# Linear attention and gated feed-forward on one core: the first chunk taken alone, and other tiles for the norms and first folds

## The chip, the cores and the metric

The kernel runs on one core of one Trainium2 chip. The metric is the device time of one execution in microseconds (us). The kernel before took 1321.6 us, the median of three runs (1320.43 to 1321.61 us).

## The reference

The input is x, 8 chunks of 512 tokens with 512 features. Every token is normalised, the attention branch forms three projections and a running sum over the tokens, the feed-forward branch runs between Hadamard transforms (fwht), and the two meet in a gate:

```python
xn = (x - mean) / sqrt(var + 1e-5)
q, k, v = xn @ Wq.T + bq, xn @ Wk.T + bk, xn @ Wv.T + bv
phi_q, phi_k = elu(q) + 1, elu(k) + 1
s = (phi_q * cumsum(phi_k * v, tokens)) * SCALE @ Wo.T + bo
y = fwht(xn * SU_ug) / 64
h = silu(y @ W_gate.T * ws_gate * 64) * (y @ W_up.T * ws_up * 64)   # 2048 wide
z = (fwht(h * SU_dp) / 64) @ W_down.T * (ws_down * 64)
out = x + s * silu(z)
```

## The kernel before

The eight chunks are taken in four pairs (`PAIRS`). Operands are split into two float16 halves, HI and LO, and a product is the sum of HI·HI, HI·LO and LO·HI, so that the result is near float32. The Hadamard transforms are folded into the weights of gate, up and down, on the chip, while the first pair runs.

A pair runs through 22 groups: K, V, Q, K, V, Q and then eight times gate and up. A group of the first pair (`first_group`, on every engine) is four tiles of 128x512, numbered 0 to 87 through the groups as 4g + j; tile j of a group has the weight rows `ROW_OF[j]` and the chunk `CHUNK_OF[j]`. A tile of the first pair is twelve matmuls (`plain_tile`, line 1542): six with kk=0, then six with kk=1. Later pairs use seven products for a group (line 1641), in the Winograd manner. After the groups come the down products (line 1719) and the attention output (line 1751).

The order on each engine is the order of the code; semaphores tie the engines. What the change and the prediction touch:

- **SyncE** loads x of the first two chunks (line 518, four tiles each, `ident` between the chunks), then Wk, Wv and Wq (line 523), constants, and the eight blocks of gate and up (line 530).
- **VectorE** takes the statistics (lines 970 and 985), the inverse root by Newton steps (lines 995 to 1002), and normalises (line 1008). `weight_scale` (lines 949 to 1156) makes a power-of-two scale from a weight's bound; `attn_low` (line 1167) writes the LO half of a piece of weights, which is what `piece_made` counts and what a group of TensorE waits for. `first_x_low` (line 1032) writes LO of the tokens.
- **ScalarE** squares the attention weights (`square_attn`, line 673) for that bound, writes HI of a piece (`attn_high`, line 705) and HI of the tokens (`first_x_high`, line 680), squares the gate and up blocks (`square`, line 712), and takes the tiles of K and Q (exp at line 799, relu at line 802). `square(i)` has two buffers: it waits until the norm of block i-2 is done.
- **TensorE** transposes the normalised tokens (line 1677), runs the tiles, sums the squares of block i in `norm(i)` (line 1561, 16 small matmuls), and folds the Hadamard signs into gate and up (`fold(n, second)`, lines 1575 and 1577; with q = 2(n-6) + second). A tile waits until the tile four before it has been taken out of its bank.
- **Bounds and folds of gate and up** on VectorE: `read_norms` (line 1207), after all eight norms; `scale_gate_up` (lines 1218 to 1223); the additions of the transform, `fly_rows` (lines 1259 and 1260, 1.2 us each); `fold_low` (line 1268), the LO half of what TensorE folds; `scale_hidden` (lines 1228 to 1240); `ug_low` (line 1174), the LO half of a folded piece. The HI halves are ScalarE's `fold_high` (line 742) and `ug_high` (lines 728 and 733).

At which tile each of these stands is said by tables (`FLY_AT`, `FOLD_HIGH_AT`, `FOLD_LOW_AT`) and by conditions in `first_weights` and in the two `first_group` functions. On VectorE the work of a tile is `use`: one feature for K (line 1075), product and scan for V (lines 1085 and 1090), feature and context for Q (lines 1075 and 1099).

Of the kernel before, what the change touches and what calls it, by code (L numbers as in the profile page):

```python
# [8 lines left out]
I32 = mybir.dt.int32  # L9
ALU = mybir.AluOpType  # L10
# [55 lines left out]
FIRST_TOKENS = {B11: 0, B21: 1, B12: 2, B22: 3}  # L66
# [32 lines left out]
FLY_AT = {6: (0, 0), 7: (0, 1), 10: (1, 0), 11: (1, 1)}  # L99
FOLD_HIGH_AT, FOLD_LOW_AT = {(14, 0): 0, (15, 1): 0}, {(15, 0): 0, (17, 1): 0}  # L100
for _i in range(1, FP):
    if _i >= 2:
        FLY_AT[8 * _i + 8], FLY_AT[8 * _i + 9] = (_i, 0), (_i, 1)
    FOLD_HIGH_AT[8 * _i + 11, 0], FOLD_HIGH_AT[8 * _i + 15, 1] = _i, _i
    FOLD_LOW_AT[8 * _i + 13, 0], FOLD_LOW_AT[8 * _i + 16, 1] = _i, _i

# [61 lines left out]
def build(nc, x, x_t, wk_t, wv_t, wq_t, wo_t, ug_t, down_t, vecs, rows, ident_in, hada_in, signs_in, out):  # L168
# [6 lines left out]
    with ExitStack() as ctx_stack:  # L175
# [111 lines left out]
        x_made, x_ready = sem("x_made"), sem("x_ready")  # L287
# [123 lines left out]
        def tile_in(eng, p, g, j):  # L411

            if p == 0:
                eng.wait_ge(plain_done, 4 * g + j + 1)
                return plain_bank(g, j)[:, :]
            if j == C21:
                eng.wait_ge(product_done, products_to(p, g, P4))
                return chain_bank(g)[:, :]
            eng.wait_ge(summed, 3 * nth(p, g) + (1, 2, 0, 3)[j])
            return tile(g, j)  # L420

        @block.sync
        def _(sp):
# [92 lines left out]
            for c in FIRST_CHUNKS:  # L516
                for t in range(TB):
                    sp.dma_start(x_ln[:, TB * c + t, :], x[c, t * P:(t + 1) * P, :]) \
                        .then_inc(x_first_loaded[TB * c + t], 16)
                if c == FIRST_CHUNKS[0]:  # L520
                    sp.dma_start(ident[:, :], ident_in).then_inc(ident_loaded, 16)
            for m, w in ((K, wk_t), (V, wv_t), (Q, wq_t)):
                sp.dma_start(raw_attn[m], w).then_inc(attn_raw_loaded[m], 16)
                if m == K:
                    sp.dma_start(vec[:, :], vecs).then_inc(vec_loaded, 16)
# [54 lines left out]
        def _(pool):  # L580
# [3 lines left out]
            def rstd_of(p):  # L584
                pool.wait_ge(var_ready, p)
                pool.tensor_tensor(rstd[:, :], var_eps[:, :], minus_half[:, :], ALU.pow).then_inc(rstd_ready, 1)
# [48 lines left out]
            for m in (K, V, Q):  # L635
                pool.wait_ge(attn_squared, m + 1)
                all_max(m, m + 1).then_inc(attn_bounded, 1)
            load_blocks(0)
# [29 lines left out]
        def _(act):  # L668
# [7 lines left out]
            def first_x_high(a):  # L676
                kk, b = FIRST_BLOCKS[a]
                act.wait_ge(xp_done, 4 if a < 4 else 8)
                src = bank[(R_BANK if kk else D_BANK)[FIRST_TOKENS[b]]]
                act.activation(xops[:, kk, HI, b, :], src[:, :], ACT.Copy).then_inc(x_hi, 1)  # L680
# [154 lines left out]
            def first_group(g):  # L835
                for j in range(4):
# [11 lines left out]
                    if j in (1, 3) and QKV_GROUPS <= g + 2 < GROUPS:  # L848
                        ug_high(g + 2, j // 2)
# [37 lines left out]
            for a in range(8):  # L887
                first_x_high(a)
            square_attn(V)
            square_attn(Q)  # L890
            attn_high(1)
# [33 lines left out]
        def _(dve):  # L925
# [41 lines left out]
            def first_stats():  # L967
                for t in [TB * c + t for c in FIRST_CHUNKS for t in range(TB)]:
                    dve.wait_ge(x_first_loaded[t], 16)
                    last = dve.bn_stats(stats[:, t, :], x_ln[:, t, :])  # L970
                prep.after(last)
                variances(0)
# [10 lines left out]
            def variances(p):  # L983
                for t in range(2 * TB):
                    last = dve.bn_aggr(mean_var[:, t, :], stats[:, t, :])
                prep.after(last)
                last = dve.tensor_scalar(var_eps[:, :], mean_var[:, :, 1], EPS, None, ALU.add)
                if p:
                    last.then_inc(var_ready, 1)
                else:  # L990
                    prep.after(last)

            def first_inverse_root():

                prep.after(dve.tensor_scalar(newton[:, :].bitcast(I32), var_eps[:, :].bitcast(I32), 1, None,
                                             ALU.logical_shift_right))
                prep.after(dve.tensor_scalar(rstd[:, :].bitcast(I32), newton[:, :].bitcast(I32), -1.0,
                                             float(INVERSE_ROOT_BITS), ALU.mult, ALU.add))
                for _ in range(NEWTON_STEPS):
                    prep.after(dve.scalar_tensor_tensor(newton[:, :], rstd[:, :], -0.5, rstd[:, :], ALU.mult, ALU.mult))  # L1000
                    prep.after(dve.tensor_tensor(newton[:, :], newton[:, :], var_eps[:, :], ALU.mult))
                    prep.after(dve.scalar_tensor_tensor(rstd[:, :], newton[:, :], 1.5, rstd[:, :], ALU.add, ALU.mult))

            def scale_root():
                prep.after(dve.tensor_scalar(rstd[:, :], rstd[:, :], X_SCALE, None, ALU.mult))

            def normalise(t):
                dve.tensor_scalar(x_ln[:, t, :], x_ln[:, t, :], mean_var[:, t, 0:1], rstd[:, t:t + 1],
                                  ALU.subtract, ALU.mult).then_inc(xn_ready, 1)

            def means_and_roots(p):
                dve.wait_ge(rstd_ready, p)
                if p > 1:
                    dve.wait_ge(mean_root_stored, 16 * (p - 1))
                dve.tensor_scalar(mean_root[:, 0, :], mean_var[:, :, 0], 1.0, None, ALU.mult)
                prep.after(dve.tensor_scalar(mean_root[:, 1, :], rstd[:, :], X_SCALE, None, ALU.mult))  # L1016
                dve.sem_inc(mean_root_made, 1)
# [10 lines left out]
            def first_x_low(a):  # L1028
                kk, b = FIRST_BLOCKS[a]
                src = bank[(R_BANK if kk else D_BANK)[FIRST_TOKENS[b]]]  # L1030
                dve.wait_ge(x_hi, a + 1)
                last = dve.tensor_tensor(xops[:, kk, LO, b, :], src[:, :], xops[:, kk, HI, b, :], ALU.subtract)  # L1032
                if a % 4 == 3:
# [352 lines left out]
            def first_weights(g, part):  # L1386
# [3 lines left out]
                if g == 2 and part == 3:  # L1390
                    read_norms()
                if 4 * g + part in FLY_AT:
                    i, level = FLY_AT[4 * g + part]
                    fly_rows(i, level)
                if g == 3:
                    if part == 1:
                        scale_gate_up()
                    elif part == 3:
                        fold_low(0, 0)
                        scale_hidden()  # L1400
                else:
                    for m in range(2):
                        if (4 * g + part, m) in FOLD_LOW_AT:
                            fold_low(FOLD_LOW_AT[4 * g + part, m], m)
                if part == 0 and QKV_GROUPS <= g + 1 < GROUPS:
                    ug_low(g + 1, True)
                if part == 2 and QKV_GROUPS <= g + 2 < GROUPS:
                    ug_low(g + 2, False)
# [59 lines left out]
            first_stats()  # L1468
            first_inverse_root()
            scale_root()  # L1470
            for t in range(TB):
                normalise(TB * FIRST_CHUNKS[0] + t)
            weight_scale(K)
            for t in range(TB):
                normalise(TB * FIRST_CHUNKS[1] + t)
            attn_low(0)
            for a in range(8):
                first_x_low(a)
            weight_scale(V)
            attn_low(1)  # L1480
# [55 lines left out]
        def _(pe):  # L1536
            def plain_tile(g, j):
# [3 lines left out]
                for n, (kk, dh, s, xs) in enumerate(terms):  # L1541
                    mm = pe.matmul(plain_bank(g, j)[:, :], at[:, s, 2 * dh + kk, r, :],  # L1542
# [48 lines left out]
            def first_group(g):  # L1591
                pe.wait_ge(piece_made, g + 1)
                for j in range(4):
                    if g == 0 and j < 2:
                        pe.wait_ge(x_ready, j + 1)
                    wait_plain_bank(g, j)
                    plain_tile(g, j)
                    n = 4 * g + j - (2 if g == 0 else 3)
                    if (2 if g else 0) <= n < FP:
                        norm(n)  # L1600
                    if QKV_GROUPS <= g + 2 < GROUPS and j in (0, 2):
                        fold(g + 2, j // 2)
# [67 lines left out]
            def first_transposes():  # L1670
                for a, c in enumerate(FIRST_CHUNKS):
                    for t in range(TB):
                        pe.wait_ge(xn_ready, TB * a + t + 1)
                        for k in range(KB):
                            dh, kk = divmod(k, 2)
                            to = bank[(R_BANK if kk else D_BANK)[2 * c + dh]]
                            mm = pe.transpose(to[:, t * P:(t + 1) * P], x_ln[:, TB * c + t, k * P:(k + 1) * P],
                                              ident[:, :])
                            if t == TB - 1:
                                mm.then_inc(xp_done, 1)  # L1680
# [76 lines left out]
            first_transposes()  # L1757
# [62 lines left out]
```

## Time and profile before

| | |
|---|---|
| median of three runs | 1321.6 us |
| profiled execution | 1322.33 us |
| its span | 1320.5 us |
| TensorE busy, matmul | 1283.2 us (97%) |
| VectorE busy | 887.5 us (67%) |
| ScalarE busy | 542.6 us (41%) |
| GpSimd busy | 63.1 us (5%) |
| mean granted TensorE clock | 0.996 |

Busy shares are means over stages with different limits. The span starts with the first instruction and the rest of the time, 1.8 us, lies around it. The times of the timeline are from the span's start. An engine's idle time stands in brackets behind the instruction that ended it, with what released it.

### The profile page before, as it was taken

What the parts mean: (1) busy time and instruction counts of PE and PEld (TensorE: products, weight loads), DVE (VectorE), ACT (ScalarE), POOL (GpSimd) and SP (SyncE); (2) the same over time, 40 slices, a digit from 0 to 9 for tenths busy, and PEclk for the clock granted to TensorE, in tenths of its full rate; (3) what the DMA queues carried; (4) which work ended last, traced back from release to release, by engine and by line L of the source; (5) the groups of instructions that cost most, each with busy time, mean ns of one, the idle gap of its engine ahead of it and who ended that gap; (6) DMA issues with size and microseconds to landing.
All of it is one profiled execution on the core that took longest, in us unless ns stands there. A gap on an engine that the chain in (4) does not pass through costs nothing.

```text
span 1320.5 us, 15902 instructions
## 1 busy us (share of the span) xinstructions
PE 1283.2 (97%) x6004; PEld 581.5 (44%) x6004; DVE 887.5 (67%) x1367; ACT 542.6 (41%) x819; POOL 63.1 (5%) x108
## 2 busy tenths in 40 slices
PE   4989999999999999999999999999999999999998
PEld 3434444444444444444444444444444444444443
DVE  6889999978776777767725755566754674455423
ACT  5855665640125655441114554442112654443000
POOL 1000111121000010110000000010000000000000
PEclk9989999999999999999999999999999999999999
DMA  9512443578765366644545323334444323323230
GB/s 364 231 56 88 175 158 145 181 245 307 186 261 178 126 212 234 204 148 132 208 140 191 128 96 128 119 136 160 159 160 162 126 100 124 128 98 126 98 126 32
DMA packets 54508, 210.44 MB, mean 159 GB/s; under 512 B 12064, under 2 KB 12320, under 8 KB 37792
## 3 DMA queue, kind: packets, MB, share of 16 engines
q1 hardware_dynamic: 45888, 180.07, 38.4%
q0 software_dynamic: 8544, 29.37, 6.7%
q8 instruction: 47, 0.77, 0.2%
q14 instruction: 29, 0.24, 0.1%
HBM read 164.30 MB, written 45.11 MB: 159 GB/s over the span
## 4 chain that ended last, share of the span: by engine, by line
PE 57%; DVE 3%; issue 2%; ACT 2%; DMA 1%; DVEq 0%; ACTq 0%
PE bank L1641 34%; PE bank L1719 19%; PE bank L1751 4%; DMA h_all<-scr_f 1%; ACT work L799 1%; DVE work L1085 1%; ACT work L802 1%; DVE work L1069 0%; DVE work L1108 0%; DVE work L1075 0%; DVE h_all L1117 0%; ACT h_all L756 0%; ACT work L789 0%; ACT L799 0%; DVE h_all L1202 0%
## 5 line engine op out<-in xcount | busy, mean ns | idle before, releaser
L1641 PE MATMUL bank<-xops,ring 128*128 128x512 f16 x2772 | 602.7, 379 | 7.5 <-DVE work L1069 2.9
L1641 PEld LDWEIGHTS bank<-xops,ring 128*128 128x128 f16 x2772 | 269.5, 98 | 339.7 <-issue 9.8
L1719 PE MATMUL bank<-ring,h_all 128*128 128x512 f16 x1536 | 333.3, 379 | 1.4 <-DMA ring<-scr_d 1.4
L1069 DVE TENSOR_TENSOR work<-bank,work 128x512 f32<-128x512 f32 x198 | 133.8, 686 | 164.7 <-PE bank L1641 150.9
L1542 PE MATMUL bank<-xops,ring 128*128 128x512 f16 x1056 | 239.4, 382 | 5.0 <-DVE xops L1032 2.7
L1719 PEld LDWEIGHTS bank<-ring,h_all 128*128 128x128 f16 x1536 | 150.2, 98 | 182.9 <-DMA ring<-scr_d 1.9
L789 ACT ACTIVATE work<-bank 128x512 f32<-128x512 f32 x198 | 117.8, 595 | 243.9 <-PE bank L1641 243.2
L1542 PEld LDWEIGHTS bank<-xops,ring 128*128 128x128 f16 x1056 | 103.1, 98 | 135.4 <-issue 14.8
L883 ACT ACTIVATE gate_g<-gate_g 128x512 f32<-128x512 f32 x32 | 19.9, 630 | 252.3 <-DVE gate_g L1349 252.3
L819 ACT ACTIVATE h_all<-work 128x512 f16<-128x512 f32 x128 | 77.9, 624 | 68.6 <-DVE work L1108 68.3
L1349 DVE TENSOR_TENSOR gate_g<-bank,row 128x512 f32<-128x512 f32 x32 | 21.4, 688 | 115.6 <-PE bank L1719 115.0
L1117 DVE TENSOR_TENSOR h_all<-work,h_all 128x512 f16<-128x512 f32 x128 | 87.4, 686 | 5.9 <-ACT h_all L819 4.7
L1751 PE MATMUL bank<-ring,ctx 128*128 128x512 f16 x384 | 84.2, 379 | 0.0
L1075 DVE SCALAR_TENSOR_TENSOR work<-work 128x512 f32<-128x512 f32 x64 | 44.1, 690 | 57.0 <-ACT work L802 56.8
L1751 PEld LDWEIGHTS bank<-ring,ctx 128*128 128x128 f16 x384 | 37.6, 98 | 45.3
L812 ACT ACTIVATE work<-bank,gate_out 128x512 f32<-128x512 f32 x56 | 38.0, 683 | 37.4 <-PE bank L1542 37.3
L812 ACT ACTIVATE work<-work,gate_out 128x512 f32<-128x512 f32 x72 | 51.0, 714 | 5.4 <-DVE work L1069 5.1
L1108 DVE SCALAR_TENSOR_TENSOR work<-work,up_out 128x512 f32<-128x512 f32 x72 | 52.2, 744 | 0.7 <-DVE mean_root L1016 0.4
L1108 DVE SCALAR_TENSOR_TENSOR work<-bank,up_out,work 128x512 f32<-128x512 f32 x56 | 41.8, 746 | 16.0 <-PE bank L1641 11.4
L1090 DVE TENSOR_TENSOR_SCAN work<-work 128x512 f32<-128x512 f32 x32 | 39.2, 1224 | 1.1
L799 ACT ACTIVATE work<-work,vec,i_attn 128x512 f32<-128x512 f32 x36 | 29.1, 807 | 9.6 <-DVE work L1069 9.5
L1358 DVE SCALAR_TENSOR_TENSOR s_f<-bank,o_out,row 128x512 f32<-128x512 f32 x32 | 23.9, 747 | 11.6 <-PE bank L1751 11.6
(172 smaller groups left out, 868.9 us busy)
## 6 DMA issues: line engine op xcount, KB each, us to landing
ring<-scr_g SPq DMA_DIRECT2D x66, 1024.0 KB, 4.8
ring<-scr_d SPq DMA_DIRECT2D x32, 1024.0 KB, 5.0
scr_g<-ring SPq DMA_DIRECT2D x22, 512.0 KB, 2.7
h_all<-in_ug_t SPq DMA_DIRECT2D x8, 1024.0 KB, 15.0
x_res<-in_x SPq DMA_DIRECT2D x32, 256.0 KB, 3.9
out<-x_res SPq DMA_DIRECT2D x32, 256.0 KB, 6.9
scr_g<-ring POOLq DMA_DIRECT2D x12, 512.0 KB, 4.1
work<-in_x_t SPq DMA_DIRECT2D x6, 1024.0 KB, 7.3
```

Of the source, the lines that this page charges most:

```text
L789: act.activation(tile(g, j), chain_bank(g)[:, :], ACT.Copy).then_inc(copied, 1)
L799: act.activation(exp_tile(n), src, ACT.Exp, bias=vec[:, b + f:b + f + 1], scale=i_attn[:, m:m + 1])
L812: act.activation(tile(g, j), src, ACT.Silu, scale=gate_out[:, at:at + 1]).then_inc(act_tiles, 1)
L819: act.activation(h[:, i, TILE_OF[j], HI, :], tile(g, j), ACT.Copy).then_inc(h_hi, 1)
L1069: dve.tensor_tensor(tile(g, j), at[:, :], tile(g, j), ALU.add).then_inc(summed, 1)
L1075: dve.scalar_tensor_tensor(tile(g, j), exp_tile(n), 1.0, tile(g, j), ALU.min, ALU.add) \
L1108: dve.scalar_tensor_tensor(tile(g, j), src, up_out[:, at:at + 1], tile(g - 1, j), ALU.mult, ALU.mult).then_inc(h_made, 1)
L1117: dve.tensor_tensor(at[:, LO, :], tile(g, j), at[:, HI, :], ALU.subtract).then_inc(h_ready, 1)
L1542: mm = pe.matmul(plain_bank(g, j)[:, :], at[:, s, 2 * dh + kk, r, :], xops[:, kk, xs, PLAIN_B[dh][c], :], start=(n == 0), stop=(n == len(t ...
L1641: mm = pe.matmul(to[:, :], weight_of(slot, s, b, kk), xops[:, kk, xs, c, :], start=(a == 0 and m in (P1, P2, P5)), stop=(a == 5), skip_gro ...
L1719: mm = pe.matmul(bank[D_BANK[t]][:, :], at[:, s, cols], w[:, :, ws, :], start=(a == 0 and b == 0 and n == 0), stop=(a == KB - 1 and b == K ...
L1751: mm = pe.matmul(bank[R_BANK[t]][:, :], at[:, s, cols], o_weight(slot)[:, f, ws, :], start=(n == 0), stop=(n == 3 * KB - 1))
```

## The change

**Loads.** SyncE issues the first chunk's four tiles, `ident`, then Wk, and only then the second chunk's four tiles, `vec`, Wv and Wq.

**First chunk alone.** VectorE takes the statistics of chunk 0 only, its inverse root, and normalises it; the scale of Wk; then the statistics of chunk 1, `attn_low(0)`, the LO halves of chunk 0, and only then normalises chunk 1. The inverse root of chunk 1 is a power on GpSimd, as in later pairs. TensorE transposes chunk 0 and runs tile 0; then it transposes chunk 1 into the same banks (4 to 7 for both, `X_BANKS`) and runs the rest of group 0 in the order 2, 1, 3. Tile 0 starts when the kk=0 half of its tokens is there (`x_half`). ScalarE's HI halves of chunk 1 stand behind the squares of Wv and Wq.

**Other tiles.** The norms stand behind tiles 3, 4, 6, 8, 9, 10, 11, 12 (before: 2, 3, 5, 6, 7, 8, 9, 10); `read_norms` at tile 9 (11), `scale_gate_up` at 10 (13), the first level of `fly_rows` of block 1 at 11 (10) and the second at 13 (11), `fold_low` of block 0 at 12 and 16 (15 and 17), its `fold_high` at 12 and 14 (14 and 15), `scale_hidden` at 14 (15). The first two folds on TensorE stand behind tiles 17 and 18 (16 and 18), `ug_high` of them at 18 and 19 (17 and 19), `ug_low` at 19 and 20 (18 and 20). From q = 2 on nothing moves.

```diff
-FIRST_TOKENS = {B11: 0, B21: 1, B12: 2, B22: 3}
+X_BANKS = {(0, B11): 4, (1, B11): 5, (0, B21): 6, (1, B21): 7, (0, B12): 4, (1, B12): 5, (0, B22): 6, (1, B22): 7}
+FIRST_ORDER = (0, 2, 1, 3)
...
-FOLD_HIGH_AT, FOLD_LOW_AT = {(14, 0): 0, (15, 1): 0}, {(15, 0): 0, (17, 1): 0}
+FOLD_HIGH_AT, FOLD_LOW_AT = {(12, 0): 0, (14, 1): 0}, {(12, 0): 0, (16, 1): 0}
...
+NORM_AT = (3, 4, 6, 8, 9, 10, 11, 12)
...
+            load_first_x(FIRST_CHUNKS[0])
+            sp.dma_start(ident[:, :], ident_in).then_inc(ident_loaded, 16)
+            sp.dma_start(raw_attn[K], wk_t).then_inc(attn_raw_loaded[K], 16)
+            load_first_x(FIRST_CHUNKS[1])
+            sp.dma_start(vec[:, :], vecs).then_inc(vec_loaded, 16)
+            for m, w in ((V, wv_t), (Q, wq_t)):
                 sp.dma_start(raw_attn[m], w).then_inc(attn_raw_loaded[m], 16)
...
             square_attn(K)
             attn_high(0)
-            for a in range(8):
+            for a in range(4):
                 first_x_high(a)
             square_attn(V)
             square_attn(Q)
+            for a in range(4, 8):
+                first_x_high(a)
             attn_high(1)
...
+            def normalise(c):
+                at = slice(TB * c, TB * c + TB)
+                if c == FIRST_CHUNKS[1]:
+                    dve.wait_ge(rstd_ready, 1)
+                prep.after(dve.tensor_scalar(rstd[:, at], rstd[:, at], X_SCALE, None, ALU.mult))
+                for t in range(TB * c, TB * c + TB):
+                    dve.tensor_scalar(x_ln[:, t, :], x_ln[:, t, :], mean_var[:, t, 0:1], rstd[:, t:t + 1],
+                                      ALU.subtract, ALU.mult).then_inc(xn_ready, 1)
...
-            first_stats()
+            first_stats(FIRST_CHUNKS[0])
             first_inverse_root()
-            scale_root()
-            for t in range(TB):
-                normalise(TB * FIRST_CHUNKS[0] + t)
+            normalise(FIRST_CHUNKS[0])
             weight_scale(K)
-            for t in range(TB):
-                normalise(TB * FIRST_CHUNKS[1] + t)
+            first_stats(FIRST_CHUNKS[1])
             attn_low(0)
-            for a in range(8):
+            for a in range(4):
                 first_x_low(a)
+            normalise(FIRST_CHUNKS[1])
             weight_scale(V)
+            for a in range(4, 8):
+                first_x_low(a)
...
+                    if g == 0 and j < 2 and n in (0, 6):
+                        pe.wait_ge(x_ready if kk else x_half, j + 1)
...
-                    if g == 0 and j < 2:
-                        pe.wait_ge(x_ready, j + 1)
                     wait_plain_bank(g, j)
-                    plain_tile(g, j)
-                    n = 4 * g + j - (2 if g == 0 else 3)
-                    if (2 if g else 0) <= n < FP:
-                        norm(n)
-                    if QKV_GROUPS <= g + 2 < GROUPS and j in (0, 2):
-                        fold(g + 2, j // 2)
+                    plain_tile(g, j if g else FIRST_ORDER[j])
+                    if g == 0 and j == 0:
+                        first_transposes(FIRST_CHUNKS[1])
+                    if 4 * g + j in NORM_AT:
+                        norm(NORM_AT.index(4 * g + j))
+                    if 4 * g + j in FOLD_AT:
+                        fold(QKV_GROUPS + FOLD_AT[4 * g + j] // 2, FOLD_AT[4 * g + j] % 2)
```

Line numbers differ in the changed kernel; what a line is can be told by its operands. ScalarE at the start of the program, before: ctx is the raw Wk and Wv, x_res the raw Wq, bank to xops the HI halves of the tokens, ring the weight pieces, s_f and gate_g the squares of gate and up.

```order
L673 ACTIVATE ring,amax<-ctx 128x2048
L705 ACTIVATE ring<-ctx,s_attn 128x1024
L680 ACTIVATE xops<-bank 128x512 x8
L673 ACTIVATE ring,amax<-ctx 128x2048
L673 ACTIVATE ring,amax<-x_res 128x2048
L705 ACTIVATE ring<-ctx,s_attn 128x1024
L712 ACTIVATE s_f<-h_all 128x2048
```

And now:

```order
L689 ACTIVATE ring,amax<-ctx 128x2048
L721 ACTIVATE ring<-ctx,s_attn 128x1024
L696 ACTIVATE xops<-bank 128x512 x4
L689 ACTIVATE ring,amax<-ctx 128x2048
L689 ACTIVATE ring,amax<-x_res 128x2048
L696 ACTIVATE xops<-bank 128x512 x4
L721 ACTIVATE ring<-ctx,s_attn 128x1024
L728 ACTIVATE s_f<-h_all 128x2048
```

Four of the eight HI halves moved behind the two squares. TensorE from its first instruction, before (ident rows are transposes, 128x512 rows tiles of twelve, ones rows norms):

```order
L1677 MATMUL bank<-ident,work 128x128 x32
L1542 MATMUL bank<-xops,ring 128x512 x36
L1561 MATMUL bank<-ones,s_f 128x1 x16
L1542 MATMUL bank<-xops,ring 128x512 x12
L1561 MATMUL bank<-ones,gate_g 128x1 x16
L1542 MATMUL bank<-xops,ring 128x512 x24
L1561 MATMUL bank<-ones,s_f 128x1 x16
L1542 MATMUL bank<-xops,ring 128x512 x12
L1561 MATMUL bank<-ones,gate_g 128x1 x16
```

And now:

```order
L1697 MATMUL bank<-ident,work 128x128 x16
L1565 MATMUL bank<-xops,ring 128x512 x12
L1697 MATMUL bank<-ident,work 128x128 x16
L1565 MATMUL bank<-xops,ring 128x512 x36
L1584 MATMUL bank<-ones,s_f 128x1 x16
L1565 MATMUL bank<-xops,ring 128x512 x12
L1584 MATMUL bank<-ones,gate_g 128x1 x16
L1565 MATMUL bank<-xops,ring 128x512 x24
L1584 MATMUL bank<-ones,s_f 128x1 x16
L1565 MATMUL bank<-xops,ring 128x512 x24
L1584 MATMUL bank<-ones,gate_g 128x1 x16
```

A tile stands between the two halves of the transposes, and each norm stands one or two tiles later. VectorE from `attn_low(4)` of tile 9 on, before:

```order
L1167 SCALAR_TENSOR_TENSOR ring<-ctx,s_attn,ring 128x1024
L1075 SCALAR_TENSOR_TENSOR work<-work 128x512
L1099 TENSOR_TENSOR ctx<-work 128x512
L1259 TENSOR_TENSOR xops<-h_all 128x4x256
L1260 TENSOR_TENSOR xops<-h_all 128x4x256
L1075 SCALAR_TENSOR_TENSOR work<-work 128x512
L1099 TENSOR_TENSOR ctx<-work 128x512
L1207 TENSOR_SCALAR norms<-bank 128x32
```

And now:

```order
L1193 SCALAR_TENSOR_TENSOR ring<-ctx,s_attn,ring 128x1024
L1233 TENSOR_SCALAR norms<-bank 128x32
L977 TENSOR_SCALAR norms<-norms 128x32
L978 TENSOR_SCALAR norms<-norms 128x32
L981 TENSOR_REDUCE amax<-vec 128x1
L1239 TENSOR_REDUCE amax<-norms 128x2
L1101 SCALAR_TENSOR_TENSOR work<-work 128x512
L1125 TENSOR_TENSOR ctx<-work 128x512
```

The reading of the norms moved ahead of the additions of block 1 and of the work of tiles 10 and 11; nothing was added or taken away here.

## Rows read from the trace of the kernel before

**Rows 1.** Waits of TensorE in the whole span: total us, times, longest.
```profile
PE bank L1575 <- DVE h_all L1268: 3.8, 1, 3.8
```

**Rows 2.** Busy time by stretch: stretch, its length, busy us (instructions) by engine, clock.
```profile
100.00:110.00 10.00, 8.35 (x37) 3.60 (x35) 9.90 (x11) 6.91 (x12) 0.00 (x0) 1.00 0.01 2
...
200.00:260.00 60.00, 60.00 (x270) 27.17 (x269) 58.35 (x89) 35.30 (x60) 6.69 (x10) 1.00 0.39 144
```

**Rows 3.** The page: GB/s in 40 slices of 33 us.
```profile
GB/s 364 231 56 88 175 158 145 181 245 307 186 261 178 126 212 234 204 148 132 208 140 191 128 96 128 119 136 160 159 160 162 126 100 124 128 98 126 98 126 32
```

**Rows 4.** Timeline to 31 us: start, us, what, [idle before it and releaser].
```profile
6.37 4.12 DVE L970 BATCH_NORM_STATS2 stats<-work 128x6 f32<-128x512 f32 x6 [1.43 <-DMA work<-in_x]
...
10.53 0.64 DVE L985 BATCH_NORM_AGGREGATE mean_var<-stats 128x2 f32<-128x6 f32 x8
...
12.34 1.91 ACT L673 ACTIVATE ring<-ctx 128x2048 bf16<-128x2048 f32 x1 [10.33 <-DMA ctx<-in_wk_t]
...
13.83 1.94 DVE L1008 TENSOR_SCALAR work<-work,mean_var,rstd 128x512 f32<-128x512 f32 x4
...
14.52 5.15 PE L1677 MATMUL bank<-ident,work 128*128 128x128 f32 x32 [14.52 <-DVE work L1008]
...
15.69 0.14 DVE L949 TENSOR_SCALAR pw<-amax_all 128x1 f32<-128x1 f32 x1
...
16.68 1.15 ACT L705 ACTIVATE ring<-ctx,s_attn 128x1024 f16<-128x1024 f32 x1 [2.34 <-DVEq L1161]
...
17.96 4.03 ACT L680 ACTIVATE xops<-bank 128x512 f16<-128x512 f32 x8
18.57 1.28 DVE L1167 SCALAR_TENSOR_TENSOR ring<-ctx,s_attn,ring 128x1024 f16<-128x1024 f32 x1
19.76 4.87 DVE L1032 TENSOR_TENSOR xops<-bank,xops 128x512 f16<-128x512 f32 x8
...
22.39 7.93 PE L1542 MATMUL bank<-xops,ring 128*128 128x512 f16 x36 [2.72 <-DVE xops L1032]
...
25.86 1.13 ACT L705 ACTIVATE ring<-ctx,s_attn 128x1024 f16<-128x1024 f32 x1
...
30.50 0.76 ACT L799 ACTIVATE work<-bank,vec,i_attn 128x512 f32<-128x512 f32 x1
```

**Rows 5.** GpSimd's power (line 586): ns min/median/max, first and last start.
```profile
L586 POOL TENSOR_TENSOR rstd<-var_eps,minus_half x3: 1669/1694/1847, 320.3 to 882.9; 128x8 f32<-128x8 f32 x3
```

**Rows 6.** The transposes alone (line 1677) by stretch: TensorE busy, weight loads, clock.
```profile
15.00:16.00 1.00, 1.00 (x6) 1.00 (x5) 1.00 0.99 418
...
18.00:19.00 1.00, 1.00 (x12) 1.00 (x11) 1.00 1.06 418
```

**Rows 7.** Timeline from 38 to 55 us.
```profile
38.80 0.69 DVE L1075 SCALAR_TENSOR_TENSOR work<-work 128x512 f32<-128x512 f32 x1 [2.44 <-ACT work L802]
...
45.34 1.91 ACT L712 ACTIVATE s_f<-h_all 128x2048 bf16<-128x2048 f32 x1 [1.08 <-PE bank L1561]
...
49.44 1.26 DVE L1167 SCALAR_TENSOR_TENSOR ring<-ctx,s_attn,ring 128x1024 f16<-128x1024 f32 x1
```

**Rows 8.** Timeline from 70 to 90 us: VectorE's idle times, TensorE's tiles.
```profile
71.65 0.69 DVE L1075 SCALAR_TENSOR_TENSOR work<-work 128x512 f32<-128x512 f32 x1 [2.02 <-ACT work L802]
...
74.42 7.60 PE L1542 MATMUL bank<-xops,ring 128*128 128x512 f16 x24
...
79.52 0.75 DVE L1085 SCALAR_TENSOR_TENSOR work<-bank,bv_in,work 128x512 f32<-128x512 f32 x1 [0.95 <-PE bank L1542]
...
82.29 5.34 PE L1542 MATMUL bank<-xops,ring 128*128 128x512 f16 x24
...
89.15 0.69 DVE L1075 SCALAR_TENSOR_TENSOR work<-work 128x512 f32<-128x512 f32 x1 [2.00 <-ACT work L802]
```

**Rows 9.** Busy time by stretch: TensorE's idle time at the first fold, its clock.
```profile
72.50:73.00 0.50, 0.00 (x0) 0.00 (x0) 0.50 (x1) 0.15 (x1) 0.00 (x0) 0.50 0.00 0
```

**Rows 10.** Timeline at 110 us: the start of tile 28.
```profile
110.65 2.76 PE L1542 MATMUL bank<-xops,ring 128*128 128x512 f16 x12 [2.31 <-DVE ring L1174]
```

## What the change will do to the time: the prediction

> **What bounds the kernel now.** I read the waits of TensorE first. In 1320.5 us it is idle only here and there, and most of that in the first 111 us: until its first transpose at 14.52, 2.7 us before the first tile, 3.8 us before the first fold [rows 1, 4], 2.3 us before tile 28 [rows 10]. The reader should see that each wait ends on VectorE. The stretches come next: after tile 28 TensorE is busy 60.00 of 60.00 us from 200 to 260, VectorE 58.35 [rows 2]. So from tile 28 on TensorE is the bound, and whatever moves the start of tile 28, or slows TensorE after it, moves the end. The edit ends before that point. Before it the bound is another one: VectorE is busy 9.90 of the 10 us before 110 [rows 2], and tile 28 was released by its `ug_low` [rows 10]. The timeline shows that VectorE has no idle time between the feature of tile 3 at 38.80 and the feature at 71.65, and then three: 2.02, 0.95 and 2.00 us, the last at 89.15, tile 20 [rows 7, 8]. I therefore keep a ledger of VectorE from 38.80 to tile 28: the same instructions in another order, plus or minus idle time.
>
> **Step 1, the start.** Before, eight statistics ended at 10.49 and normalising began at 13.83 [rows 4]. With four tiles the third still starts at 6.37, the fourth ends at 7.75 (0.69 each), and the 3.34 us behind it shrink by half of the aggregates' 0.64: normalising starts at 10.8 and gives way to the scale of Wk 1.86 later, at 12.65. Wk landed at 12.34 behind 1 MB of x more; at 364 GB/s [rows 3] 1 MB is 2.9 us, so 9.5. Its square takes 1.91, and the scale began at most 1.44 after the square before, so 12.8 at the latest: I take 12.7. From there the old distances [rows 4]: `attn_high(0)` 0.99 later (13.7), HI of the tokens 1.28 after that (15.0), four of them at 0.50 end at 17.0. VectorE has the scale until 13.65, four statistics (2.75), aggregates and epsilon (0.5), which makes 16.9; `attn_low(0)` takes 1.19, two LO halves 1.2, and TensorE follows 0.2 later: tile 0 starts at about 19.5, not 22.39. That is a gain of 2.9 us for tile 0. The wait of 2.7 us goes, but the transposes of chunk 0 start at 11.5, end near 14, and the next wait is 5.5 us.
>
> GpSimd's power for chunk 1 has from 16.9 until VectorE is through with the LO halves at 20.6. Later in the program that operation takes 1.67 to 1.85 us on twice the columns [rows 5], so it costs nothing: the LO halves and `attn_low(0)` cover 3.7 us. If that cover went, each us beyond it would be passed on.
>
> **Step 2, what tile 0 holds up.** Chunk 1 is normalised from 20.8 to 22.7 and TensorE transposes it only after tile 0. ScalarE has done its four HI halves at 17.0 and the two squares at 20.9 (3.87 before, from 21.99 to 25.86), and then waits for the transposes. At full clock tile 0 takes 12 x 0.22 = 2.6 us and 16 transposes at 12 per us 1.35 us [rows 4, 6]: 23.5. At half clock the two would lose up to 3.9 us more.
>
> Which clock? In the row of 72.50 to 73.00 it is 0.50, granted in a wait of 3.8 us [rows 1, 9]; the waits of 2.7 and 2.3 us left it at 1.00. A wait of 5.5 us after 2.5 us of transposes is beyond both, so I take half clock (1.2 GHz), given back during tile 0 or the transposes: a loss of 2.1 us, from bounds of 0 and 3.9. The transposes end at 25.6. One row speaks of the same thing at the start: the clock column has 1.00 from 15 to 16, yet 6 transposes ran in that us and 12 in the one from 18 to 19 [rows 6], at a pace below the 8 per us that normalising fed.
>
> The Trainium skill (TensorE: Matmul & The Clock Gate, "Part 1: The HAM clock gate") says that 1.2 GHz is the level of an idle array and the default, and full clock comes only with sustained work. The column of this trace disagrees (1.00 throughout the first 60 us), the pace of the transposes agrees. By the column alone the loss of 2.1 us would be none; by the page tile 0 runs slow whatever came before.
>
> ScalarE then writes four HI halves (2.0) until 27.6, and the distance from there to exp of tile 0 was one `attn_high` and two squares, 30.50 - 25.86 = 4.64: 32.3 instead of 30.50, later by 1.8. At full clock it would be 30.2, earlier by 0.3. ScalarE is without a pause from there to relu of tile 3, so VectorE's feature of tile 3 moves from 38.80 to about 40.6.
>
> **Step 3, the later norms.** `square(5)` needs norm 3 and `square(6)` norm 4, now behind tiles 8 and 9 instead of 6 and 7. TensorE's tiles take 2.6 us (24 in a row: 5.34 for two [rows 8]), a norm 0.4 more. After 25.6 come eight tiles (2, 1, 3, 4 to 8) and norms 0 to 3: 25.6 + 20.8 + 1.6 = 48.0; tile 9 and norm 4: 51.0. `square(6)` starts at 51.2 (45.34 before), takes 1.91, and `attn_high(3)` behind it 1.1: 54.2. VectorE would have reached `attn_low(3)` at 49.44 + 1.8 = 51.2 [rows 7]. So it waits 3 us that it did not wait, and does `attn_low(3)` 4.75 us later than before. At full clock this is 2.65, as all of it hangs on 25.6.
>
> Behind it I find no other new wait up to tile 20. `read_norms` needs norm 7 behind tile 12, at 60.2; VectorE comes to it at 61.7 (`attn_low(3)`, 2.4 of transform, two Q tiles, `attn_low(4)`). Margin 1.5 us; from there a later norm would be paid in full. The bound's maximum on GpSimd lies beside tile 10.
>
> **Step 4, the stalls that go.** `fold_low(0, 0)` is done at about 71, and TensorE, after 17 tiles, asks for it at 73: the 3.8 us wait goes, and with it the half clock. Its price is in the rows: the two tiles behind that fold took 7.60 us against 5.34 for the next two [rows 8], 2.3 more. But neither was on VectorE's path. What the ledger gets back is VectorE's own idle time: 2.02 (relu held by `fold_high`, which waited for the scale), 0.95 (tile 17 at half clock) and 2.00 (tile 20 not there). Now tile 17 runs at full clock from 70, and tile 20 is done at about 83, six us before VectorE comes to it at 89, so all three go: 4.97.
>
> **Sum.** Tile 28: +1.8 +2.95 -4.97 = -0.2 us, 110.4 instead of 110.65. TensorE, now ahead, comes to the end of tile 27 near 104.4 and has but one fold of the down rows to do until 110.4: some 5 us idle in 6, in two pieces of which the longer is over 3 us. That lies beyond the 2.3 us that kept the clock and near the 3.8 that lost it. I expect half clock again, and the price that it had at the first fold, 2.3 us, now at a place where TensorE is the bound. Bounds: 0, if the clock holds, and about 3.5, if it comes back later than there. Total +2.1 us: 1324.4 for an execution like the profiled one (its span of 1320.5 and 1.8 around it make 1322.33), which lay 0.7 above the median; against 1321.6 it is 1323.7.
>
> **Rivals.**
> - *The clock holds before tile 28.* Same ledger, no 2.3: -0.2, 1321.4. For it: two pieces, neither as long as 3.8. Against: hardly anything done between. 17%.
> - *Tile 0 at full clock*, as the column would have it: ledger -2.3, tile 28 at 108.4, and with the half clock behind it no change, 1321.6; without it 1319.3. Against: 5.5 us idle. 10%.
> - *The end gets the stalls back: faster.* If the squares do not hold up `attn_low(3)`, because ScalarE has them done or TensorE's norms come earlier than I add up, the ledger loses its 2.95: -3.2. The half clock may still cost its 2.3. That gives 1318.4 without it and 1320.7 with it. It decides from a wait below 0.3 us before `attn_low(3)`. For it: the sum of eight tiles is mine. Against: the order of norm and square is fixed. 15%.
> - *Chunk 1 comes later: slower.* GpSimd's power or the landing of Wk is late by 1 to 2 us, and tile 0 is followed by later HI halves: +1.5 on top, 1325.2. 10%.
>
> **Chances and range.** The forecast has 48%. The measurement can tell 0.2%, 2.6 us, so faster is below 1319.0 and slower above 1324.2. My forecast lies just inside; its own spread is about 1.2 us either way (1322.5 to 1324.9), 20 of its 48 are slower. With the late start's 10, and 6 for a longer half clock or a second one, slower has 36%. Faster has 20: most of the third rival without the half clock, part of the second, and 8 for a ledger wrong by more than I see. The same: 44%. Range 1318.2 to 1326.3.
>
> **What would show it.** Step 1: the first tile near 19.5. Step 2: its matmuls at 0.43 us, the transposes of chunk 1 ending at 25 to 26, exp of tile 0 at 32. Step 3: a VectorE wait of 3 us before `attn_low(3)`, released by ScalarE. Step 4: no TensorE wait before the first fold, and none of the three idle times of VectorE. Sum: tile 28 at 110 to 111, with a clock of 0.50 behind it. The prediction is wrong if tile 28 starts before 108, or if TensorE shows idle time between there and the end of the pair that it did not have.

## The result, and the profile after

The changed kernel takes 1331.52 us, the median of five runs (1327.49 to 1332.26), against 1320.43 us of the kernel before in the same session: the ratio is 1.0076, with a 95% interval of 1.0066 to 1.0087. It is slower by some 10 us. The forecast was +2.1 us, with a range up to 1326.3.

The profiled execution has a span of 1330.0 us, 9.5 more than before. The waits of TensorE in the first 300 us, in total, times, longest (tiles are line 1565 now, folds 1598 and, for down, 1610; weight pieces come from `ug_low`, line 1200):

```profile
PE bank L1697 <- DVE work L1032: 11.8, 1, 11.8
PE bank L1565 <- DVE xops L1056: 9.2, 2, 4.7
PE bank L1565 <- DVE ring L1200: 3.1, 1, 3.1
PE bank L1598 <- DVE h_all L1294: 1.5, 1, 1.5
PE bank L1610 <- DVE ring L1316: 1.5, 1, 1.5
PE bank L1565 <- DVE work L1111: 0.9, 1, 0.9
```

The wait of 3.8 us before the first fold [rows 1] is gone. There are two waits of over 4 us for the tokens' LO halves where one of 2.7 us was, and the one before tile 28 has grown from 2.3 to 3.1 us. The timeline of the start says what stands behind them. These rows answer to [rows 4, 7, 10]:

```profile
10.01 1.91 ACT L689 ACTIVATE ring<-ctx 128x2048 bf16<-128x2048 f32 x1 [8.01 <-DMA ctx<-in_wk_t]
...
12.21 0.83 POOL L603 PARTITION_ALL_REDUCE amax_all<-amax  x1 [11.38 <-ACT ring L689]
...
19.75 5.28 PE L1565 MATMUL bank<-xops,ring 128*128 128x512 f16 x12 [4.49 <-DVE xops L1056]
...
21.65 1.05 POOL L600 TENSOR_TENSOR rstd<-var_eps,minus_half 128x4 f32<-128x4 f32 x1 [8.61 <-issue]
...
22.74 0.17 DVE L1030 TENSOR_SCALAR rstd<-rstd 128x4 f32<-128x4 f32 x1 [1.94 <-POOL rstd L600]
...
31.11 0.72 POOL L603 PARTITION_ALL_REDUCE amax_all<-amax  x2 [8.40 <-issue]
31.52 0.15 DVE L967 TENSOR_SCALAR pw<-amax_all 128x1 f32<-128x1 f32 x1 [6.66 <-POOL amax_all L603]
...
34.18 7.64 PE L1565 MATMUL bank<-xops,ring 128*128 128x512 f16 x24 [4.68 <-DVE xops L1056]
...
37.43 0.76 ACT L815 ACTIVATE work<-bank,vec,i_attn 128x512 f32<-128x512 f32 x1
...
45.74 0.69 DVE L1101 SCALAR_TENSOR_TENSOR work<-work 128x512 f32<-128x512 f32 x1 [2.44 <-ACT work L818]
...
62.42 1.28 DVE L1193 SCALAR_TENSOR_TENSOR ring<-ctx,s_attn,ring 128x1024 f16<-128x1024 f32 x1 [5.63 <-ACT ring L721]
...
118.25 5.30 PE L1565 MATMUL bank<-xops,ring 128*128 128x512 f16 x12 [3.07 <-DVE ring L1200]
```

GpSimd (POOL) finishes the maximum for Wk at 13.04 and begins the power at 21.65. Its operands were there at 17.2; between the two the profile shows nothing that it waited for ("issue"). The power ends at 22.70, and the next maximum, for Wv, begins at 31.11, 8.40 us later, though ScalarE had its operand ready at 19.2. GpSimd's configuration instructions (`MODIFY_POOL_CONFIG`) show the change from one kind of instruction to the other. At the lines of the power and the maximum there are six and four now, where the kernel before had four (from 309.0 on) and two (up to 0.9); the new ones stand from 12.6 to 23.0:

```profile
L600 POOLq MODIFY_POOL_CONFIG  x6: 37/44/83, 12.6 to 875.8; - x6
L603 POOLq MODIFY_POOL_CONFIG  x4: 1/6/11, 0.8 to 23.0; - x4
```

VectorE stands from 24.9 to 31.52 for the maximum of Wv, and behind its scale of Wv, in its own queue, stand the LO halves of chunk 1, for which TensorE stands until 34.18. Exp of tile 0 comes at 37.43 (30.50 before), the feature of tile 3 at 45.74 (38.80), `attn_low(3)` at 62.42 (49.44), tile 28 at 118.25 (110.65), and that tile runs at half clock, as the busy times by stretch say (clock is the third column from the end). So do tiles 1 and 3 behind the wait of 4.68 us: 24 matmuls in 7.64 us, 5.34 at full clock.

```profile
34.00:38.00 4.00, 3.82 (x10) 1.34 (x11) 3.19 (x9) 4.00 (x3) 0.90 (x2) 0.50 0.68 243
...
118.00:120.00 2.00, 1.75 (x5) 0.65 (x6) 1.69 (x11) 0.00 (x0) 0.00 (x0) 0.50 0.49 195
```

VectorE's ledger closes with these rows: the feature of tile 3 is 6.94 us late, the wait before `attn_low(3)` adds 5.63, the three idle times give back 4.97, and that makes the 7.60 us by which tile 28 is late. Tile 28 takes 5.30 instead of 2.76 us; tile 29 starts at 124.19 instead of 113.68, 10.5 us late. About 1 us comes back later: one kind of wait for VectorE in the later pairs (line 1108 before, 1134 now) is 2.0 instead of 2.8 us in all, and the one for the down weights' transfer 1.2 instead of 1.4.

### The profile page after: what moved, and what is told of

The parts are those of the page before. It is cut to its first block, busy times and chain, and to the rows that moved or that the text cites. A ratio compares the mean times of both kernels' runs of the same rounds, so it can differ in the third digit from the quotient of the medians.

```text
span 1330.0 us, 15909 instructions
## 1 busy us (share of the span) xinstructions
PE 1289.1 (97%) x6004; PEld 582.7 (44%) x6004; DVE 887.7 (67%) x1369; ACT 542.4 (41%) x819; POOL 64.0 (5%) x109
## 4 chain that ended last, share of the span: by engine, by line
PE 56%; DVE 3%; issue 2%; ACT 2%; DMA 2%; DVEq 0%; ACTq 0%
PE bank L1663 33%; PE bank L1739 19%; PE bank L1771 4%; DMA h_all<-scr_f 2%; ACT work L815 1%; DVE work L1111 1%; ACT work L818 1%; DVE work L1095 0%; DVE work L1134 0%; DVE work L1101 0%; DVE h_all L1228 0%; DVE h_all L1143 0%; ACT h_all L772 0%; DVE h_all L1215 0%; ACT work L805 0%
```

## Experiments

The theory (switch) was that GpSimd pays some 8.5 us each time it goes from the maximum across partitions to an ordinary instruction or back; the rest of my ledger holds. The rivals were that the power is slow itself or held by its operands, and that the norms, the tables or the half clock cost the 10 us. An edit is shown by its main lines.

**The power replaced by Newton steps.**

```diff
-                if m == K:
-                    rstd_of(0)
...
-                    dve.wait_ge(rstd_ready, 1)
+                first_inverse_root(c)
```

> The changed kernel with the inverse root of chunk 1 by Newton steps on VectorE (11 small instructions, some 2.2 us) in place of the power on GpSimd. Theory (switch): GpSimd pays some 8.5 us whenever it goes from the maximum to the power or back, so the bound of Wv comes 7 us late; without the power the scale of Wv starts at 25 to 27 instead of 31.5, VectorE's attn_low(3) at 55.5 instead of 62.4, tile 28 at 111 to 112 instead of 118.2, and the time is 6 to 7 us below the changed kernel, near 1325. Rival (the norms and the half clock do it, the power only waits for something that is late anyway): the scale of Wv stays near 31, the time within 2 us of 1331.5.

1321.93 us, ratio to before 1.0007 (0.9999 to 1.0016): the loss is gone, some 9 us of it. From the timeline of that run, the maximum for Wv, the scale of Wv, the tiles 2, 1 and 3, `attn_low(3)` and tile 28:

```profile
18.71 0.35 POOL L602 PARTITION_ALL_REDUCE amax_all<-amax  x1 [6.30 <-ACT ring L686]
...
24.86 0.14 DVE L964 TENSOR_SCALAR pw<-amax_all 128x1 f32<-128x1 f32 x1
...
25.48 7.93 PE L1557 MATMUL bank<-xops,ring 128*128 128x512 f16 x36
...
54.22 1.28 DVE L1186 SCALAR_TENSOR_TENSOR ring<-ctx,s_attn,ring 128x1024 f16<-128x1024 f32 x1 [2.91 <-ACT ring L718]
...
110.02 5.30 PE L1557 MATMUL bank<-xops,ring 128*128 128x512 f16 x12 [3.07 <-DVE ring L1193]
```

The maximum now follows the square at once. `attn_low(3)` waits 2.91 us, where the prediction had 2.95, and tile 28 starts at 110.0, where it had 110.4. The theory's 111 to 112 was too late by 1, and its time, near 1325, too long by 3. Without the switch TensorE has no second wait at the start, and the 36 matmuls behind the transposes of chunk 1 ran in 7.93 us, at full clock.

**An unused power, and an unused addition, in the kernel before.** Nothing waits for either; the only other addition is the setting of its constant at the very start.

```diff
                 all_max(m, m + 1).then_inc(attn_bounded, 1)
+                if m == K:
+                    pool.tensor_tensor(unused[:, :], halves[:, :], minus_half[:, :], ALU.add if ADD else ALU.pow)
```

> The kernel before, and on GpSimd, between the maximum for Wk and that for Wv, a power of a constant whose result nothing reads; nothing waits for it and it waits for nothing. Theory (switch): it starts about 8.5 us after the maximum for Wk, near 23.5, the maximum for Wv follows near 33, and the scale of Wv moves from 24.55 to about 33.5; half of it is taken up by idle time of VectorE (5 us), so 3.5 to 8 us slower than before. Rival (the power was held by its operands in the changed kernel, or by VectorE at a shared port): it starts at once, 1.7 us, and nothing moves, 0 us.

> As e2_unused_power with an addition in the place of the power. Theory (the change between the maximum across partitions and an ordinary instruction costs, whatever the instruction): the addition starts 8 to 10 us after the maximum for Wk, the maximum for Wv 8 us after it, the time 10 us above the kernel before. Rival (only the power has to be fetched): it starts at once, and the time is that of the kernel before, within 1 us.

The power: 1331.43 us, ratio 1.0078 (1.0066 to 1.0091). The addition: 1328.77 us, 1.0059 (1.0045 to 1.0073). GpSimd's timeline with the addition:

```profile
14.31 0.52 POOL L592 PARTITION_ALL_REDUCE amax_all<-amax  x1 [13.44 <-ACT ring L678]
...
25.34 0.19 POOL L642 TENSOR_TENSOR unused<-halves,minus_half 128x8 f32<-128x8 f32 x1 [10.51 <-issue]
...
33.91 0.72 POOL L592 PARTITION_ALL_REDUCE amax_all<-amax  x2 [8.38 <-issue]
```

An addition of 0.19 us costs 7 to 8 us of the kernel's time (I had expected 10), because it stands between two maxima: 10.51 us before it, 8.38 behind it (10.54 and 7.92 with the power). So it is the switch and not the power, and it has nothing to do with this change's chunks or tables. I had expected 3.5 to 8 us for the power, and measured 10.4. Its trace has three things that I had not counted: the scale of Wv came at 35.03 instead of 33.5, of VectorE's three idle times 2.02 us before the feature of tile 15 and 0.43 before that of tile 20 stayed, and tile 28, 7.8 us late, ran in 4.23 us instead of 2.76, partly at half clock, behind a wait of 2.31 us.

**The old norms.** As the first experiment, with

```diff
-NORM_AT = (3, 4, 6, 8, 9, 10, 11, 12)
+NORM_AT = (2, 3, 5, 6, 7, 8, 9, 10)
```

> As e1_newton_both, and the norms behind the tiles of the kernel before (2, 3, 5, 6, 7, 8, 9, 10). Theory (squares held by norms): the wait before attn_low(3), released by ScalarE, falls from about 3 us to under 1, tile 28 starts 2.5 to 3 us earlier than in e1_newton_both, and the time is 2.5 to 3 us below it, near 1322. Rival (VectorE is not what sets tile 28): no difference to e1_newton_both, under 1 us.

1321.26 us, ratio 0.9995 (0.9986 to 1.0004). VectorE has no wait at `attn_low(3)` and tile 28 starts at 108.14, 1.9 us earlier; from the feature of tile 3 on it is 66.40 us instead of 69.42, 3.0 less, as this execution was 1.1 us later up to there. In the medians only 0.7 us of it shows, within what the intervals leave open (0.9995 and 1.0007 lie 1.6 us apart, their bounds overlap). The mechanism is shown by the trace, the size of its gain in time is not.

**The tables alone**, norms included, with the first chunk taken as before:

> The kernel before with the other tiles alone (norms, read_norms, scale_gate_up, fly_rows, fold_high, fold_low, scale_hidden, the first two folds with ug_high and ug_low); the first chunk is taken as before. Theory (ledger of VectorE): attn_low(3) at 53.5 instead of 49.44, VectorE's idle time of 5 us before tile 20 gone, tile 28 at about 109.8, and half clock behind it (2.3 us): +1.4 us on the kernel before, if the clock holds -0.9. Rival (TensorE's stall of 3.8 us and the slow tiles behind the first fold come back in full): 5 to 6 us faster than before.

1321.61 us, ratio 1.0007 (0.9999 to 1.0016). Timeline: `attn_low(3)` and tile 28.

```profile
53.34 1.28 DVE L1175 SCALAR_TENSOR_TENSOR ring<-ctx,s_attn,ring 128x1024 f16<-128x1024 f32 x1 [3.75 <-ACT ring L713]
...
109.15 4.82 PE L1545 MATMUL bank<-xops,ring 128*128 128x512 f16 x12 [3.07 <-DVE ring L1182]
```

53.3 against 53.5 expected. The 3.8 us stall of TensorE is gone and nothing comes of it: VectorE's later norms eat most, the half clock the rest.

**The first chunk alone**, Newton steps for both chunks, every table as before:

> The part of the change on the first chunk alone, with Newton steps for both chunks, and every table (norms, bounds, folds) as in the kernel before. Theory (ledger): VectorE's feature of tile 3 at 41.7 (38.80 before), its idle times before tile 20 stay, since TensorE moves less than VectorE: tile 28 at 113 to 114, time 2.5 to 3 us above the kernel before, near 1324. Rival (the earlier tile 0 is worth its 2.8 us, and what costs is the tables): 2 to 3 us below the kernel before.

1321.61 us, ratio 1.0008 (0.9999 to 1.0017). Timeline: the first fold, VectorE at tile 20, tile 28.

```profile
75.35 0.61 PE L1587 MATMUL bank<-xops,signs 128*128 128x512 f16 x1 [4.85 <-DVE h_all L1279]
...
91.15 0.69 DVE L1086 SCALAR_TENSOR_TENSOR work<-work 128x512 f32<-128x512 f32 x1 [2.00 <-ACT work L807]
...
112.65 2.76 PE L1554 MATMUL bank<-xops,ring 128*128 128x512 f16 x12 [2.31 <-DVE ring L1185]
```

Tile 0 starts 3.2 us earlier than before (19.21) and tile 28 2.0 us later. The first fold waits 4.85 instead of 3.8 us. The time rose by about 1 us by the ratio, 2.2 at most; I expected 2.5 to 3. In the profiled execution the span is 1.3 us longer than before, so 0.7 of the 2.0 came back behind tile 28, as with the changed kernel.

**Keeping the clock.** Matmuls that nothing reads, in TensorE's idle time, on the third experiment's kernel: 5 behind tile 27, 13 before tile 28.

```diff
+            def fill(to, n):
+                for _ in range(n):
+                    pe.matmul(to[:, :], signs[:, :], xops[:, 0, HI, B11, :], start=True, stop=True)
...
+                if g == QKV_GROUPS + 1:
+                    fill(plain_bank(g, 0), 13)
                 pe.wait_ge(piece_made, g + 1)
```

> As e3_newton_old_norms, and TensorE does 5 matmuls of 128x512 behind tile 27 and 13 before its wait for the weights of tile 28, into the bank that tile 28 then starts anew; their results are read by nothing. They are 3.9 us of work in some 4.3 us of idle time. Theory (the half clock behind tile 28 is granted for the idle time before it, and TensorE is the bound there): clock 1.00, tile 28 takes 2.75 us instead of 5.30 and starts when it did (108.1), and the time is 2.3 to 2.6 us below e3_newton_old_norms, near 1318.8. Rival (TensorE has slack behind tile 28): the clock holds and the time does not move, under 0.5 us. Rival (the matmuls delay tile 28): the time rises.

1316.93 us, ratio 0.9971 (0.9959 to 0.9982).

```profile
104.40 2.97 PE L1608 MATMUL bank<-xops,signs 128*128 128x512 f16 x13
107.63 2.76 PE L1557 MATMUL bank<-xops,ring 128*128 128x512 f16 x12 [0.26 <-DVE ring L1193]
```

Tile 28 takes 2.76 us at a granted clock of 1.00, and the time is some 3 us below the third experiment's (by the two ratios, 0.24%): TensorE is the bound there, and the half clock cost what it took. The clock column has 1.00 in the whole execution, yet tile 0, behind a wait of 4.45 us, took 4.91 us: at the start the column does not say what ran, as with the first transposes [rows 6].

With 20 unread matmuls of 128x256 besides, between the transposes of chunk 0 and tile 0:

> As e6_fill_before_tile28, and 20 matmuls of 128x256 between the transposes of chunk 0 and tile 0, results read by nothing. Theory (tile 0 at half clock holds up the transposes of chunk 1 and with them ScalarE): tile 0 takes 2.75 us instead of 5.28, the transposes of chunk 1 end near 25.5 (bound by normalising) instead of 26.6, exp of tile 0 and VectorE's feature of tile 3 come 1.1 us earlier, and the time falls by 1.1 us more. Rival: no more than 0.3 us, since normalising chunk 1 sets it anyway.

1316.40 us, ratio 0.9966 (0.9952 to 0.9980), against 0.9971: no difference that can be told. Tile 0 took 2.75 us, and exp of tile 0 came at 32.37 instead of 32.87; the transposes waited 1.26 us for normalising. 0.40 of that half microsecond was there before the added matmuls (first transposes at 11.12 instead of 11.52). So the rival was right: once Newton steps stand in VectorE's queue there, tile 0's half clock is worth next to nothing.

**The same in the kernel before**, 16 matmuls before the first fold:

> The kernel before, and 16 matmuls of 128x512 on TensorE before its wait for the first fold, results read by nothing: 3.5 us of work in 3.8 us of idle time. My prediction said that the slow tiles behind the first fold were on VectorE's path only by idle times of 0.95 and 2.00 us. Theory (ledger): clock 1.00 behind the fold, those two idle times gone, tile 28 2.5 to 3 us earlier, the time 2 to 3 us below the kernel before, near 1318.3; if the clock then falls before tile 28, no gain. Rival (they are not on the path): VectorE's idle time only moves elsewhere, 0 us.

1317.33 us, ratio 0.9977 (0.9968 to 0.9985).

```profile
75.03 0.39 PE L1575 MATMUL bank<-xops,signs 128*128 128x512 f16 x1 [1.41 <-DVE h_all L1268]
...
87.94 0.69 DVE L1075 SCALAR_TENSOR_TENSOR work<-work 128x512 f32<-128x512 f32 x1 [0.43 <-ACT work L802]
...
109.44 4.41 PE L1542 MATMUL bank<-xops,ring 128*128 128x512 f16 x12 [2.30 <-DVE ring L1174]
```

The fold is fast, VectorE's idle time of 0.95 us is gone and that of 2.00 us is 0.43. Slow tiles behind a stall cost some 3 us here although the engine that they belong to was not the bound: the bound engine waited for two of them. The last line bears on the prediction: the wait before tile 28 is as long as in the kernel before (2.30 and 2.31 us), where the clock stayed at 1.00; here it fell to 0.50, and tile 28 took 4.41 us. This execution took 1320.01 us, the longest of eleven, of which eight took 1316.1 to 1318.2.

**In the changed kernel as it is**, the 5 and 13 matmuls:

> The changed kernel as it is, and the 5 and 13 unread matmuls of e6_fill_before_tile28. Theory (of its 10 us, 7.5 are the later tile 28 and the rest is half clock behind it): tile 28 at 118 as before, in 2.75 us instead of 5.30, the time 2.3 to 2.6 us below the changed kernel, near 1329. Rival: no change.

1327.52 us, ratio 1.0045 (1.0032 to 1.0057), against 1.0076: 4 us, more than expected. Tile 28 is fast, and in this execution it also starts at 115.81, since `attn_low(3)` stood at 60.01 instead of 62.42. The added matmuls come later than that, so this part is no effect of theirs. GpSimd's two switches took 11.30 and 6.84 us here, 8.61 and 8.40 in the changed kernel's profile, but their sum is nearly the same, and the scale of Wv (31.39) and the feature of tile 3 (45.62) come within 0.13 us of it. What differs is the clock of tiles 1 and 3:

```profile
34.06 5.35 PE L1565 MATMUL bank<-xops,ring 128*128 128x512 f16 x24 [2.84 <-DVE xops L1056]
...
60.01 1.28 DVE L1193 SCALAR_TENSOR_TENSOR ring<-ctx,s_attn,ring 128x1024 f16<-128x1024 f32 x1 [3.67 <-ACT ring L721]
```

Here they ran at full clock behind a wait of 2.84 us, the norms behind them came 2.4 us earlier, and with them the squares and `attn_low(3)`. How often that happens in the five runs of either kernel, and so how much of the 4 us is due to it, was not settled.

**A version that beats the kernel before and the changed one.** The first chunk as before, the tables of the change with the old norms, 3 unread matmuls behind tile 27 and 7 before tile 28:

> A version meant to beat both: the first chunk as in the kernel before, the norms behind their old tiles, the other tables of bounds and folds of the change, and 3 and 7 unread matmuls on TensorE behind tile 27 and before tile 28. Theory (ledger): VectorE's feature of tile 3 at 38.8 instead of 41.2 as in e6_fill_before_tile28, none of the idle times of 2.02, 0.95 and 2.00, so tile 28 near 105.5, clock 1.00, time 2 us below e6: 1314.5 to 1315.5. Rival (TensorE has become the bound before tile 28): tile 28 near 107, no gain on e6 and its 1316.9.

1315.13 us (1314.31 to 1315.50), ratio to the kernel before 0.9951 (0.9938 to 0.9963). That it is faster than 1316.93 is likely and not shown: the two ratios' intervals overlap.

```profile
40.11 0.69 DVE L1083 SCALAR_TENSOR_TENSOR work<-work 128x512 f32<-128x512 f32 x1 [2.44 <-ACT work L810]
...
106.52 2.76 PE L1545 MATMUL bank<-xops,ring 128*128 128x512 f16 x12 [1.56 <-DVE ring L1182]
```

Tile 28 is 1 us later than I said because that whole execution began 1.3 us later (feature of tile 3 at 40.11 instead of 38.80). From there on it is 66.41 us, against 71.85 in the kernel before: the 5 us of the ledger, and 0.5 more. In the execution with 5 and 13 unread matmuls, which takes the first chunk alone, it was 66.41 too (107.63 less 41.22).

## Why the prediction was wrong

**Step 1, the start: the times right, one cost missing.** Tile 0 started at 19.75 (19.5 predicted), and the square of Wk at 10.01 (9.5). The failed sentence is that GpSimd's power "costs nothing", because 3.7 us of VectorE's work covered its 1.7. I priced the instruction by a row [rows 5] whose three executions each stand behind 11.27 to 16.68 us in which GpSimd waited for the operands, long enough to hide a switch, and looked only at who waits for its result. I did not ask what stands behind it in GpSimd's own queue: the maximum for Wv, and in front of it a switch each way. They took 8.61 and 8.40 us in the changed kernel's trace, 7.92 to 10.54 in the experiments with an unused instruction.

The Trainium skill (GPSIMD Engine Reference, "2.1 Instruction dispatch") states that the first call of a freshly loaded kernel pays a load of about 6 us of which the profile shows no instruction, as the gap behind `MODIFY_POOL_CONFIG`. The runs here agree that there is such a gap with no instruction in it; its size is 6.84 to 11.30 us, more than the page's. The transfers of the start ran beside all of them (DMA share 1.01 to 1.02 from 12 to 31 us), and no run shows what a switch takes without.

**Step 2: right in kind, late by 5 us.** The power came 2 us late and the transposes of chunk 1 ended at 26.9 instead of 25.6. Tile 0 ran at half clock, as said (5.28 us), here with 0.50 in the column too. ScalarE's HI halves then ended at 29.0, but `attn_high(1)` waited for the scale of Wv until 32.78. That, not the transposes, set exp of tile 0: 37.43 instead of 32.3. The rival "chunk 1 comes later" named the power, but priced it at 1 to 2 us and looked for it at the wrong instruction.

**Step 3: the mechanism right, the size short.** The wait before `attn_low(3)`, released by ScalarE behind the later norms, was 5.63 us in the changed kernel where 2.95 was predicted, and 2.91 without the power; without the later norms it is none. The sum of eight tiles took tiles 1 and 3 at full clock. Behind the second wait, of 4.68 us, which the late scale of Wv made and which stands nowhere in the prediction, they took 2.3 us more and held up every norm.

**Step 4: right.** No TensorE wait before the first fold, and none of VectorE's three idle times. That these were all the ledger gets back is shown by the version above. One sentence in it was wrong: that neither slow tile behind the fold was on VectorE's path. They cost VectorE 0.95 and 1.57 of the 2.00 us.

**The sum.** Tile 28 at 118.25 instead of 110.4. With the power taken out it is 110.02. The half clock cost 2.5 us in tile 28 and 2.9 with the two folds behind it (2.3 predicted), at the place predicted. That the wait of 2.3 us before tile 28 "kept the clock" is true of the kernel before and no rule: three executions with that wait lost it (4.41, 4.23 and 4.03 us for tile 28). So of the miss of 8 us nearly all is one term, the power's place in GpSimd's queue, sized 0 where it cost 7.8: 5.1 us as the later feature of tile 3 (45.74 instead of 40.6), and 2.7 as the longer wait before `attn_low(3)`, most of it the slow tiles 1 and 3 (with them fast, the wait was 3.67 instead of 5.63 us).

## What to carry to other kernels

Read an engine's order for what stands behind an added instruction as well as for who waits for it, and treat a change of GpSimd between its maximum across partitions and ordinary instructions as 7 to 11 us in its queue while the first loads run, even for an instruction of 0.2 us. Keep a ledger for the engine that is busy up to the point where the bound changes hands: TensorE's stall of 3.8 us was worth nothing by itself, the 5 us of VectorE's idle time were. Where TensorE becomes the bound right behind a stall, a few unread matmuls in the stall keep the clock up: 3 us here.

## What the runs showed of the hardware

- GpSimd's switch between the maximum across partitions and an ordinary instruction shows as "issue" time without an instruction: 10.51 and 8.38 us around an addition of 0.19 us, and it does not wait for the operands: the first `MODIFY_POOL_CONFIG` for the power stands at 12.6 us, the operands were there at 17.2, and the power began at 21.65.
- TensorE's clock: idle times of 4.6 and 4.5 us before tile 0, and of 1.5 and 3.1 us around one short fold before tile 28, were followed by 1.2 GHz (12 matmuls in 5.28 and 5.30 us); with the idle time before tile 28 filled to 0.3 us it was 2.4 GHz (2.76 us).
- A wait of 2.3 us before tile 28, with the same instructions ahead of it, was followed by 2.4 GHz in two executions (2.76 us for the tile: the kernel before, the first chunk alone) and by 1.2 GHz for part of it in three (4.41, 4.23, 4.03 us: the filled first fold, the unused power, the unused addition).
- The clock column has 1.00 in the first 60 us of an execution in which tile 0 took 4.91 us instead of 2.75.
